# Every layer normalisation on VectorE as one scale and one shift per row, x's second half loaded ahead of the first expert, and a new order of all jobs

## The reference

```python
# x: (4, 1024, 128), 8 heads of 16, 8 experts with hidden size 512
def layernorm(x): return (x - mean(x)) / sqrt(var(x) + 1e-5)
n = layernorm(x)
Q, K, V = silu(n @ Wq), silu(n @ Wk), silu(n @ Wv); U = n @ Wu
scores = (Q K^T + rel_bias[s - t + 255]) / 4       # index clipped far from the diagonal
scores = where(causal and |K|.sum() != 0, scores, NEG)
x = x + (silu(scores) @ V) * silu(U)
n = layernorm(x)
gates = softmax over the 2 best of n @ w_gate.T, else 0
x = x + sum over e of gates[:, e] * ((n @ w_in[e].T) @ w_out[e].T)
```

## Time and profile before

| what | value |
|---|---|
| median of 3 runs | 328.3 us |
| the profiled execution | 330.59 us, its span 328.4 us |
| mean granted TensorE clock | 0.94 |
| busy, PE | 288.5 us, 88% |
| busy, DVE | 244.3 us, 74% |
| busy, ACT | 210.9 us, 64% |
| busy, POOL | 187.4 us, 57% |
| HBM | 109 GB/s over the span |

### The profile page before, as it was taken

How to read it: one execution, slowest core, us unless ns; L and a number is a source line. 1 busy time by engine, 2 the same in 40 slices (tenths; PEclk the granted TensorE clock), 3 DMA queues, 4 the chain that set the end, 5 groups by cost and what they waited for, 6 DMA issues and landing times.

```text
span 328.4 us, 5933 instructions
## 1 busy us (share of the span) xinstructions
PE 288.5 (88%) x1860; PEld 136.3 (42%) x1860; DVE 244.3 (74%) x767; ACT 210.9 (64%) x404; POOL 187.4 (57%) x262
## 2 busy tenths in 40 slices
PE   1688998889997999699999989999978999897591
PEld 0535543356444444243344444433434555543240
DVE  4455550672689896699999849789993997698867
ACT  1355464988995788668777868977663688663100
POOL 5293500480016899947953797287664334796672
PEclk9995585999999999999999999999996799999978
DMA  5847895026975916930396000496930010001011
GB/s 172 235 138 192 237 239 168 2 71 198 228 118 154 236 36 192 220 62 3 103 234 142 3 0 1 145 236 198 234 88 2 0 35 0 2 2 32 1 32 32
DMA packets 30669, 36.31 MB, mean 111 GB/s; under 512 B 3240, under 2 KB 17064, under 8 KB 30640
## 3 DMA queue, kind: packets, MB, share of 16 engines
q1 hardware_dynamic: 27232, 33.53, 41.4%
q10 hardware_dynamic: 3408, 2.43, 2.5%
HBM read 23.87 MB, written 12.08 MB: 109 GB/s over the span
## 4 chain that ended last, share of the span: by engine, by line
PE 55%; DVE 23%; POOL 12%; issue 5%; ACT 2%; DMA 2%; SPq 1%; DVEq 0%; POOLq 0%; ACTq 0%
PE o_acc L643 15%; PE score L626 12%; PE jobp L712 12%; DVE score L885 8%; POOL xn L401 8%; PE jobp L676 6%; DVE ymix L986 4%; PE jobp L667 2%; PE jobp L725 2%; POOL rstd L516 2%; PE jobp L684 2%; DMA xs<-in_L_attn_x 2%; PE jobp L705 2%; POOL ymix L572 2%; DVE stats L921 1%
## 5 line engine op out<-in xcount | busy, mean ns | idle before, releaser
L765 ACT ACTIVATE wts<-score 128x512 f32<-128x512 f32 (+2 forms) x200 | 100.6, 531 | 50.4 <-DVE score L885 43.9
L885 DVE TENSOR_TENSOR score<-score,bias_near 128x256 f32<-128x256 f32 (+3 forms) x288 | 113.7, 467 | 24.0 <-PE score L626 23.7
L572 POOL TENSOR_TENSOR ymix<-ymix 128x512 f32<-128x512 f32 (+2 forms) x90 | 74.4, 827 | 41.0 <-DVE ymix L986 35.5
L643 PE MATMUL o_acc<-wts,v_pad 128*32 128x512 f32 (+3 forms) x864 | 83.6, 485 | 1.3 <-ACT wts L765 1.1
L767 ACT ACTIVATE wts<-score,far 128x512 f32<-128x512 f32 x120 | 74.2, 698 | 12.9 <-DVE score L885 5.7
L712 PE MATMUL jobp<-mm_e,xn2T 128*128 128x512 f32 x120 | 66.7, 657 | 5.0 <-DVE ymix L986 3.2
L626 PE MATMUL score<-q_stack,k_stack 64*128 64x256 f32 (+3 forms) x400 | 61.8, 375 | 1.9 <-ACT wts L765 1.7
L626 PEld LDWEIGHTS score<-q_stack,k_stack 64*128 64x128 f32 x400 | 36.1, 191 | 39.5 <-issue 32.9
L986 DVE TENSOR_TENSOR ymix<-jobp,gates 128x512 f32<-128x512 f32 x60 | 40.8, 686 | 14.1 <-PE jobp L712 12.1
L401 POOL TENSOR_SCALAR xn<-xs,mv,rstd 128x128 f32<-128x128 f32 x54 | 42.7, 804 | 1.5
L712 PEld LDWEIGHTS jobp<-mm_e,xn2T 128*128 128x128 f32 x120 | 19.6, 196 | 35.7 <-issue 23.5
(11 more groups left out here) (81 smaller groups left out, 264.0 us busy)
## 6 DMA issues: line engine op xcount, KB each, us to landing
k_stack<-rows_dram SPq DMA_DIRECT2D x32, 256.0 KB, 5.2
q_stack<-rows_dram SPq DMA_DIRECT2D x28, 256.0 KB, 6.6
rows_dram<-k_hi SPq DMA_DIRECT2D x16, 256.0 KB
xs<-in_L_attn_x SPq DMA_DIRECT2D x8, 256.0 KB, 8.9
rows_dram<-k_lo SPq DMA_DIRECT2D x8, 256.0 KB
rows_dram<-q_hi SPq DMA_DIRECT2D x7, 256.0 KB
rows_dram<-q_lo SPq DMA_DIRECT2D x7, 256.0 KB
out<-xs SPq DMA_DIRECT2D x7, 256.0 KB, 7.5
```

What stands on the lines that cost most here:

```text
L572: then_wait(pool.tensor_tensor(y[:, 0:n], y[:, 0:n], y[:, n:2 * n], ALU.add))
L643: ins = pe.matmul(o_acc[32 * j:32 * j + 32, q0:q0 + n], v_pad[:, b % 2, kb, 4 * quad + j, :], wts[:, group % WTS, j, c:c + n], start=USES[ ...
L765: act.activation(weights, score[bank][:, 0:n], ACT.Silu, scale=HD ** -0.5).then_inc(weighed[bank], 1)
L885: ins = dve.tensor_tensor(score[bank][:, c + near:c + n], score[bank][:, c + near:c + n], bias, ALU.add)
```

## The change

- All 64 normalisations of a tile run on DVE, at the place of the norm job. They compute x * rstd + shift, where shift = -mean * rstd; POOL makes it with two more small products in `scale`. POOL no longer normalises at all.
- The guard against overwriting moves with it: POOL's scale waits that DVE's last normalisation has read the old rstd and shift, and DVE's stats wait that POOL has read the old mean and variance.
- SP issues x's second half ahead of expert 0.
- Every list of jobs is new. `BEFORE` is one entry that now holds V 0 1 and M 0, and no longer U 0 0. FF jobs stand earlier: up to six of them in one entry, and nine instead of twelve behind the last group. T2 stands further behind its stats2.

```diff
-def norm_on_dve(job):
-    return job[:2] == ("norm1", 0) or job == ("norm2", LAST)
...
 BEFORE = [
-    [],
-    [("stats1", 0, 0), ("RB",), ("T1", 0, 0), ("stats1", 0, 1), ("norm1", 0, 0), ("WT", 0), ("K", 0, 0),
-     ("V", 0, 0), ("split", 0, 0), ("MASK", 0, 0), ("Q", 0, 0), ("norm1", 0, 1), ("U", 0, 0)],
-    [("T1", 0, 1), ("norm1", 1, 0), ("WT", 1), ("Q", 0, 1), ("REL",), ("norm2", 0), ("K", 0, 1), ("split", 0, 1)],
+    [("stats1", 0, 0), ("RB",), ("norm1", 0, 0), ("T1", 0, 0), ("stats1", 0, 1), ("split", 0, 0), ("K", 0, 0),
+     ("WT", 0), ("MASK", 0, 0), ("norm1", 0, 1), ("V", 0, 0), ("REL",), ("WT", 1), ("split", 0, 1), ("M", 0),
+     ("Q", 0, 0), ("T1", 0, 1), ("K", 0, 1), ("Q", 0, 1), ("V", 0, 1)],
 ]
 BESIDE = [
...
+    [("U", 0, 0), ("stats1", 1, 0)],
+    [("MASK", 0, 1), ("norm1", 1, 0)],
+    [],
+    [("M", 1), ("T1", 1, 0)],
+    [("K", 1, 0)],
+    [("Q", 1, 0)],
+    [("stats2", 0), ("SEL", 0), ("split", 1, 0)],
...
+    [("M", 2), ("MASK", 1, 0)],
+    [("norm1", 1, 1), ("WT", 3), ("norm2", 0)],
+    [("T1", 1, 1)],
...
+    [("norm1", 2, 1), ("stats2", 2), ("LOG", 1), ("SEL", 2), ("best", 1, 0)],
+    [("T1", 2, 1), ("tanh", 1), ("U", 2, 0), ("best", 1, 1), ("gates", 1), ("K", 2, 1)],
...
+    [("FF", 1, 4, 0), ("best", 4, 0), ("FF", 1, 4, 1), ("T2", 4), ("FF", 1, 5, 0), ("FF", 1, 5, 1), ("LOG", 4),
+     ("FF", 1, 6, 0), ("FF", 1, 6, 1)],
...
+    [("FF", 3, 2, 0)],
+    [("FF", 3, 2, 1), ("FF", 3, 3, 0)],
 ]
 AFTER = [
...
+    [("SEL", 8)],
+    [],
+    [("norm2", 7), ("stats2", 8), ("norm2", 8), ("T2", 7), ("LOG", 7), ("best", 7, 0), ("best", 7, 1), ("T2", 8),
+     ("gates", 7), ("FF", 3, 3, 1), ("FF", 3, 4, 0), ("LOG", 8), ("FF", 3, 4, 1), ("FF", 3, 5, 0), ("tanh", 7),
+     ("best", 8, 0), ("best", 8, 1), ("FF", 3, 5, 1), ("FF", 3, 6, 0), ("gates", 8), ("FF", 3, 7, 0),
+     ("FF", 3, 6, 1), ("FF", 3, 7, 1), ("tanh", 8)],
...
-            load_expert(0)
             load_x(0, 1)
+            load_expert(0)
...
                 pool.wait_ge(averaged, n + 1)
+                if b > 0:
+                    pool.wait_ge((normed1, normed2)[ln], 1 + (unit_before(args[0]) if ln else 2 * (b - 1) + args[1]))
                 then_wait(pool.tensor_tensor(rstd[:, ln, ts], mv[:, ln, ts, 1], eps_t[:, ts], ALU.add))
-                pool.tensor_tensor(rstd[:, ln, ts], rstd[:, ln, ts], mhalf[:, ts], ALU.pow).then_inc(scaled, 1)
-                if not norm_on_dve((("norm1", "norm2")[ln],) + args):
-                    pool.wait_ge(scaled, n + 1)
-                    normalise(pool, args, ln)
+                pool.tensor_tensor(shift[:, ln, ts], mv[:, ln, ts, 0], minus[:, ts], ALU.mult)
+                then_wait(pool.tensor_tensor(rstd[:, ln, ts], rstd[:, ln, ts], mhalf[:, ts], ALU.pow))
+                pool.tensor_tensor(shift[:, ln, ts], shift[:, ln, ts], rstd[:, ln, ts], ALU.mult).then_inc(scaled, 1)
...
-                        dve.wait_ge((normed1, normed2)[ln], 1 + (unit_before(args[0]) if ln else 2 * (b - 1) + args[1]))
+                        dve.wait_ge(scaled, SCALES.index(((unit_before(args[0]),) if ln else (b - 1, args[1]), ln)) + 1)
...
-                    if norm_on_dve(job):
-                        dve.wait_ge(scaled, SCALES.index((args, ln)) + 1)
-                        normalise(dve, args, ln)
+                    b, tiles = rows_of(args, ln)
+                    dve.wait_ge(scaled, SCALES.index((args, ln)) + 1)
+                    if b > 0:
+                        wait_filled(dve, ("T2", unit_before(args[0])) if ln else ("T1", b - 1, args[1]))
+                    for t in tiles:
+                        ins = dve.tensor_scalar((xn1, xn2)[ln][:, t], xs[:, b, t], rstd[:, ln, t:t + 1],
+                                                shift[:, ln, t:t + 1], ALU.mult, ALU.add)
+                    ins.then_inc((normed1, normed2)[ln], 1)
```

More of the change, by code:

```diff
@@ L140 @@
 BEFORE = [
-    [],
[3 rows of a table removed]
[3 rows of a table added]
 ]
 BESIDE = [
-    [("V", 0, 1), ("MASK", 0, 1), ("stats1", 1, 0)],
-    [],
[L149 to L152, removed]
[22 rows of a table removed]
-    [("best", 1, 0), ("LOG", 1), ("T1", 2, 1), ("MASK", 2, 0)],
[20 rows of a table removed]
[L196 to L214, removed]
@@ L215 @@
-    [("FF", 2, 4, 0)],
-    [],
-    [],
[L218 to L224, removed]
+    [("U", 0, 0), ("stats1", 1, 0)],
+    [("MASK", 0, 1), ("norm1", 1, 0)],
+    [],
+    [("M", 1), ("T1", 1, 0)],
@@ new lines @@
+    [("K", 1, 0)],
+    [("Q", 1, 0)],
+    [("stats2", 0), ("SEL", 0), ("split", 1, 0)],
+    [("stats1", 1, 1), ("V", 1, 0)],
+    [("U", 0, 1)],
+    [("WT", 2)],
+    [("M", 2), ("MASK", 1, 0)],
+    [("norm1", 1, 1), ("WT", 3), ("norm2", 0)],
+    [("T1", 1, 1)],
+    [("WT", 4), ("T2", 0)],
+    [("Q", 1, 1), ("LOG", 0), ("best", 0, 0)],
[11 rows of a table added]
+    [("norm1", 2, 1), ("stats2", 2), ("LOG", 1), ("SEL", 2), ("best", 1, 0)],
+    [("T1", 2, 1), ("tanh", 1), ("U", 2, 0), ("best", 1, 1), ("gates", 1), ("K", 2, 1)],
@@ new lines @@
+    [("FF", 0, 4, 0), ("FF", 0, 4, 1), ("FF", 0, 5, 0), ("norm2", 2), ("FF", 0, 5, 1)],
+    [("U", 2, 1), ("V", 2, 1)],
+    [("T2", 2), ("stats1", 3, 0), ("Q", 2, 1)],
+    [("best", 2, 0), ("best", 2, 1), ("FF", 0, 6, 0), ("LOG", 2)],
+    [("split", 2, 1), ("FF", 0, 6, 1)],
+    [("FF", 0, 7, 0), ("stats1", 3, 1)],
+    [("FF", 0, 7, 1), ("norm1", 3, 0)],
+    [],
+    [],
+    [("T1", 3, 0), ("norm1", 3, 1)],
+    [("U", 3, 0), ("MASK", 2, 0), ("tanh", 2), ("gates", 2)],
+    [("K", 3, 0)],
@@ new lines @@
+    [("Q", 3, 0), ("FF", 1, 0, 0)],
+    [("SEL", 3), ("stats2", 3)],
+    [("T1", 3, 1), ("V", 3, 0)],
+    [("FF", 1, 0, 1)],
+    [("FF", 1, 1, 0), ("norm2", 3), ("split", 3, 0), ("FF", 1, 1, 1)],
+    [("MASK", 2, 1), ("FF", 1, 2, 0)],
+    [("FF", 1, 2, 1), ("T2", 3)],
+    [("stats2", 4), ("SEL", 4)],
+    [("LOG", 3), ("MASK", 3, 0)],
+    [],
+    [("best", 3, 0)],
+    [("tanh", 3), ("best", 3, 1), ("norm2", 4), ("K", 3, 1), ("FF", 1, 3, 0)],
+    [("FF", 1, 3, 1), ("gates", 3)],
+    [("FF", 1, 4, 0), ("best", 4, 0), ("FF", 1, 4, 1), ("T2", 4), ("FF", 1, 5, 0), ("FF", 1, 5, 1), ("LOG", 4),
+     ("FF", 1, 6, 0), ("FF", 1, 6, 1)],
@@ new lines @@
+    [("tanh", 4), ("best", 4, 1), ("gates", 4), ("U", 3, 1), ("FF", 1, 7, 0)],
+    [("Q", 3, 1), ("FF", 1, 7, 1)],
+    [("FF", 2, 0, 0), ("split", 3, 1)],
+    [],
+    [("FF", 2, 0, 1), ("FF", 2, 1, 0)],
+    [],
+    [("FF", 2, 1, 1)],
+    [("SEL", 5), ("V", 3, 1), ("stats2", 5)],
+    [],
+    [("FF", 2, 2, 0), ("MASK", 3, 1)],
+    [("norm2", 5), ("FF", 2, 2, 1), ("FF", 2, 3, 0)],
+    [("FF", 2, 3, 1)],
+    [("T2", 5)],
+    [("tanh", 5), ("best", 5, 0), ("best", 5, 1), ("SEL", 6), ("LOG", 5), ("gates", 5)],
@@ L225 @@
+    [("FF", 2, 4, 0), ("FF", 2, 4, 1)],
+    [("FF", 2, 5, 0), ("FF", 2, 5, 1), ("stats2", 6)],
+    [("FF", 2, 6, 0)],
+    [("FF", 2, 6, 1), ("norm2", 6), ("FF", 2, 7, 0)],
+    [("FF", 2, 7, 1)],
+    [("T2", 6)],
+    [("best", 6, 0), ("best", 6, 1), ("gates", 6), ("LOG", 6), ("SEL", 7)],
+    [("FF", 3, 0, 0), ("FF", 3, 0, 1), ("stats2", 7), ("tanh", 6)],
     [("FF", 3, 1, 0)],
     [("FF", 3, 1, 1)],
+    [("FF", 3, 2, 0)],
+    [("FF", 3, 2, 1), ("FF", 3, 3, 0)],
 ]
 AFTER = [
-    [("SEL", 8), ("stats2", 8)],
@@ L230 @@
-    [],
-    [("T2", 7)],
-    [],
[3 rows of a table removed]
-    [("gates", 8), ("FF", 3, 7, 0), ("tanh", 8), ("FF", 3, 6, 1), ("MIX",)],
     [],
@@ L239 @@
     [],
-    [("FF", 3, 7, 1)],
+    [("SEL", 8)],
+    [],
[4 rows of a table added]
+    [],
+    [],
+    [],
+    [("MIX",)],
 ]
@@ L301, in build @@
         rstd = sb("rstd", [P, 2, NT])
+        shift = sb("shift", [P, 2, NT])
         eps_t = sb("eps_t", [P, NT])
         mhalf = sb("mhalf", [P, NT])
+        minus = sb("minus", [P, NT])
         rank = sb("rank", [P, E])
@@ L392, in rows_of @@
             return b, range(f, f + tiles)
[L394 to L403, removed]
         block = ctx.enter_context(nc.Block())
@@ L455, in _ @@
             sp.dma_start(rb_s[:], rel_bias[MAXLEN - 1:, :].rearrange("(p t) h -> p t h", p=P)).then_inc(rb_in, 16)
+            load_x(0, 1)
             load_expert(0)
-            load_x(0, 1)
             sp.dma_start(far_row[:], rel_bias[2 * MAXLEN - 2:, :].to_broadcast([P, H])).then_inc(far_in, 16)
@@ L514, in scale @@
                 pool.wait_ge(averaged, n + 1)
+                if b > 0:
+                    pool.wait_ge((normed1, normed2)[ln], 1 + (unit_before(args[0]) if ln else 2 * (b - 1) + args[1]))
                 then_wait(pool.tensor_tensor(rstd[:, ln, ts], mv[:, ln, ts, 1], eps_t[:, ts], ALU.add))
-                pool.tensor_tensor(rstd[:, ln, ts], rstd[:, ln, ts], mhalf[:, ts], ALU.pow).then_inc(scaled, 1)
-                if not norm_on_dve((("norm1", "norm2")[ln],) + args):
-                    pool.wait_ge(scaled, n + 1)
-                    normalise(pool, args, ln)
+                pool.tensor_tensor(shift[:, ln, ts], mv[:, ln, ts, 0], minus[:, ts], ALU.mult)
```

(3 more changed lines are left out.)

## The result

The changed kernel takes 310.11 us (310.02 to 310.12, 4 runs), the kernel before 327.45 (326.05 to 330.67, 4 runs): a ratio of 0.9457, 95% interval 0.9383 to 0.953. The profiled execution took 310.02 us, 20.6 less than the one profiled before. The prediction was 321.5 with a range of 312 to 333: the sign was right, the size was not.

A forecast was written before the change was run, and what follows sets the result against it. The prediction took TensorE's own work to bound the body, VectorE a close second. Start −0.7, body −5.0 and tail −3.2 gave −8.9, or 321.7 against the profiled 330.6; it took 321.5 us, range 312 to 333.

The forecast's parts named there:

- Start, −0.7: Prologue and first unit: −0.4 and −0.3 us from moved work, clock effect taken as 0 (could cost 6.8 or give 12).
- the clock rival: First unit: a denser prologue keeps TensorE at 2.4 GHz longer, 6 us more gain, 315.5 us; chance 0.12.
- The walk through the prologue: Start: stepping through TensorE's list put the first transpose near 8.3 us and the first bias addition at about 24.4.
- Waits that go, −9.9 + 2.0: Body: greater distance removes TensorE's 9.9 us of waits for normalisation; two tight places cost 1.0 us each.
- the sum: Body: −9.9 + 2.0 − 5.2 + 5.0 + 3.1 = −5.0 us.
- The clock behind 248, −5.2: Body: with the 2.62 us wait gone, 10.3 us of work at 1.2 GHz takes half, −5.2 us.
- VectorE, +5.0: Body: 50 moved normalisations at 0.40 us make 20 us on VectorE; a quarter is paid, +5.0 us.
- The rivals' 90% cap: Body: strict queues allow VectorE at most a 90% busy share; used for the VectorE-bound and absorbed-gain cases.
- FF jobs and tail, +3.1 and −3.2: Three expert jobs move from tail to body, +3.1 us; last mix begins about 16.4 us after the gating, −3.2.
- The page on the shared port: Body: GpSimd and two-port VectorE operations lock each other out; a meeting at every normalisation would make 34 us, not 20.
- that rival: Body: VectorE becomes the bound, slower, 343.5 us at 0.68 us per normalisation, deciding from 0.53; chance 0.14.

The follow-up runs named there:

- e7: The kernel before with five transposes moved one entry later in the lists, nothing else: 326.33 us, ratio 1.0045.
- e9: The kernel before (engine, loads and lists) with the new lists from group 59 on: 316.11 us, ratio 0.9593.
- e13: The kernel before with six jobs of the first unit at their new places, prologue and all else as before: 319.18 us, ratio 0.9847.
- e6: The changed kernel with the old prologue contents (M 0 and V 0 1 behind the first scores, U 0 0 in the prologue): 312.99 us, ratio 0.9589.
- e10: New lists and loads with GpSimd normalising as before, but the old lists from group 59 on: 321.80 us, ratio 0.9795.
- e1: The changed kernel's new lists and load order with the old normalisation, on GpSimd except batch 0 and unit 8: 307.40 us, ratio 0.9449.
- e14: The changed kernel run once more without an edit: 310.66 us, ratio 0.9575.
- e2: The changed code, all normalisations on VectorE, with the old lists and load order, each norm job one entry behind its stats: 342.12 us, no ratio given.

## Why the prediction was wrong, by its steps

- **Start, −0.7: wrong, the term was −10.0.** The step that failed is "I take 0, since the mix of small operands and few large jobs is the same". Its ends were stated (+6.8 and −12), and the clock rival had −6; the measured value lies near the far end. Most of it is clock: 24.0 us of low clock became 3.5, an estimated 7.8 us. Against e7 and e9, whose first units are those of the kernel before, it would be −3.4 and −6.8, still far beyond −0.7. The places of six jobs are enough to hold the clock (e13), and the denser prologue that the rival named is not needed (e6). The walk through the prologue was right until 23.5 (first transpose 8.37, predicted 8.3), then missed by 0.9 us: the first bias came at 25.29, not 24.4, behind an operation on 8 columns that took 1.23 us beside GpSimd's product (0.16 in the kernel before).
- **Waits that go, −9.9 + 2.0: right in size.** Two waits of 1.0 us together are left. But a wait's length is not its worth: e7 removed 8 us of the same waits and gained nothing in the body, and in the changed kernel 5 of them went between the gatings of units 0 and 5, where nothing was gained either. TensorE's busy time there rose from 167.3 to 172.1 us with nearly the same products; why is open. So the sum came near for the body (−5.0 for −7.4) partly by luck: all of the gain lies in the last batch.
- **The clock behind 248, −5.2: too large.** The low clock is gone in the changed kernel. But the last batch with the old lists took 67.2 and 67.3 us with it (before, e10) and 66.1 in e7, which had none there: about 1 us, with two transposes moved as well.
- **VectorE, +5.0: the price was right, the charge was not.** The mean is 433 ns for 400. The body took 236.8 to 237.0 us in five profiles with VectorE and 235.9 to 236.1 in three with GpSimd, so the term measured about +0.8, all of it in the last batch. The rivals' 90% cap is not refuted: VectorE was busy 210.9 of 237.0 us, 89%, with 38.5 of 40 in one stretch. What they had wrong is the load. At 433 ns it would have been 222 us (198.6 + 2.1 + 21.7), and it was 211, since the other operations gave back 10 us in the whole run, two thirds of it by the new order (e1). The text took that relief only as a reason for the low price.
- **FF jobs and tail, +3.1 and −3.2:** three jobs fewer, the mix 16.5 us after the gating (predicted 16.4), the stage −3.1. That it agrees to 0.1 us is partly luck: in e14, the same kernel, the mix began 18.1 us after the gating and the stage took 24.3 us, −1.5, at a mean clock of 0.72 instead of 0.77. The body took the three jobs in without growing: in the last batch TensorE idles 1.8 us instead of 5.8.
- **The page on the shared port** (the Trainium skill, SBUF — State Buffer, section SBUF: two separate sides). The long operations beside GpSimd (up to 894 ns for a normalisation, 1.23 us for the 8 columns) agree with the lock that it states; that it would carry the rival was not borne out on the new order. On the old order something like that rival happened (e2), but not by the price: the normalisation took 455 ns there, against 433, and the body 259 us.

## What to carry to other kernels

Read the granted clock of each stage before pricing anything else, and treat the places of large and small matrix products in a stage at low clock as a term of its own: here six jobs were worth 5 us by the ratio, 9 by the medians. A wait in the profile is not worth its length by itself: in e7 the next product waited in its place, so ask what the list puts behind it. An engine change and a new order should be costed apart: here the order alone gave all of it, and the engine alone, with each norm job one entry behind its stats in the old order, cost 11 to 14 us. Look for the largest part stage by stage: here it was the last batch and the tail, 11 to 13 us, and not the waits that the change was priced by.

## What was not expected of the hardware

The same first unit, instruction for instruction, took 6.5 us more or less by the chance of its clock (58.2 and 51.7, with mean granted clocks of 0.64 and 0.87), and the kernel before scattered from 322.4 to 332.9 us over the sessions (one run of 831.6 aside), the changed one from 309.4 to 312.1. Why the six places hold the clock, whether by what the products fill or by when they come, is open: both lists keep TensorE busy for 93 and 94% of the stretch from 24.8 to the gating.
